# Issuing a phase's wide query product in one piece instead of one sixth per slot

## The reference, cut to what matters

```
q_hk  = (hidden_q @ Wq.T).reshape(B, S, 16, 128)
q_big = einsum('bshk,hkq->bshq', q_hk, w_kc_q)          # 192 wide per head
q_big = rope(q_big)
kv_r  = rope(kv_c)
q_r   = einsum('bshq,hqr->bhsr', q_big, W_qr)
k_r   = einsum('bld,hdr->bhlr', kv_r, W_kr)
attn  = softmax(einsum('bhsr,bhlr->bhsl', q_r, k_r))
ctx_c = einsum('bhsl,bld->bhsd', attn, kv_r)
out   = (ctx_c through w_kc_kv) @ Wo.T
```

## Time and profile before

| quantity | value |
|---|---|
| median of 3 runs | 955.08 us (953.51 to 961.84) |
| the profiled execution | 955.46 us |
| its span in the trace | 953.7 us, so 1.8 us lie around it |
| granted TensorE clock over the span | 0.93 |
| TensorE matmul busy | 847.4 us, 89% |
| VectorE, ScalarE, GpSimd busy | 61%, 44%, 47% |

### The profile page before, as it was taken

One profiled execution on the slowest core, in us unless ns is written; L12 is line 12 of the kernel. 1 busy time (PEld: TensorE's weight loads), 2 busy tenths in 40 slices (PEclk: granted clock), 3 DMA queues, 4 the chain that ended last, 5 costly groups with the idle time before them and its releaser, 6 DMA issues.

```text
span 953.7 us, 15582 instructions
## 1 busy us (share of the span) xinstructions
PE 847.4 (89%) x5844; PEld 629.2 (66%) x5844; DVE 582.8 (61%) x1112; ACT 415.9 (44%) x896; POOL 448.9 (47%) x465
## 2 busy tenths in 40 slices
PE   4998879989987799998989889899898988989884
PEld 3666756888965567766767667676676766766442
DVE  3537854222275567577587588668658748757445
ACT  2357851212121354544534544554454463454531
POOL 3000006500050187767657576666675755557530
PEclk8879989989997799999989999999999999999976
DMA  9560026589310000000000000010000000000000
GB/s 194 184 198 2 2 64 241 208 303 344 109 36 17 16 2 11 20 7 10 17 9 10 21 10 2 10 30 1 10 22 10 10 5 10 2 14 10 8 6 9
DMA packets 42167, 52.28 MB, mean 55 GB/s; under 512 B 12230, under 2 KB 35704, under 8 KB 41836
## 3 DMA queue, kind: packets, MB, share of 16 engines
q1 hardware_dynamic: 41068, 49.63, 16.6%
q0 software_dynamic: 1024, 1.64, 0.6%
HBM read 45.80 MB, written 5.36 MB: 54 GB/s over the span
## 4 chain that ended last, share of the span: by engine, by line
PE 68%; DVE 16%; ACT 7%; issue 4%; DMA 3%; POOL 1%; POOLq 0%; SPq 0%; DVEq 0%; ACTq 0%
PE ps L1167 13%; PE ps L1179 10%; PE ps L1147 7%; PE ps L1091 5%; PE ps L1015 5%; PE ps L1202 3%; PE ps L1118 3%; PE ps L969 3%; PE ps L1028 3%; PE ps L1096 2%; DVE nm L1931 2%; ACT sm L1424 2%; DMA xs<-xs_scratch 2%; DVE xyz L1902 1%; DVE h L1992 1%
## 5 line engine op out<-in xcount | busy, mean ns | idle before, releaser
L592 POOL TENSOR_TENSOR acc<-acc,pt 120x800 f32<-120x800 f32 (+1 forms) x157 | 301.6, 1921 | 123.5 <-ACT pt L1631 91.3
L1631 ACT ACTIVATE pt<-ps 120x400 f32<-120x400 f32 (+1 forms) x384 | 189.4, 504 | 237.1 <-PE ps L1167 229.4
L1931 DVE TENSOR_REDUCE nm<-ps 128x1 f32<-128x482 f32 (+1 forms) x336 | 215.7, 655 | 109.0 <-PE ps L1147 105.7
L1167 PE MATMUL ps<-qh,khl 128*120 128x400 f32 (+1 forms) x384 | 167.9, 437 | 24.0 <-ACT pt L1631 23.6
L1147 PE MATMUL ps<-khl,qh 128*128 128x482 f32 (+1 forms) x336 | 136.1, 408 | 10.6 <-DVE nm L1931 9.1
L1179 PE MATMUL ps<-pt,kv 120*64 120x400 f32 (+1 forms) x768 | 145.0, 514 | 0.0
L1167 PE MATMUL ps<-ql,kh 65*120 65x400 f32 (+1 forms) x384 | 137.2, 357 | 0.0
L1167 PEld LDWEIGHTS ps<-qh,khl 128*120 128x120 f32 (+1 forms) x384 | 72.9, 190 | 70.6 <-ACT pt L1631 34.3
L1179 PEld LDWEIGHTS ps<-pt,kv 120*64 120x64 f32 (+1 forms) x768 | 52.8, 140 | 66.6 <-issue 58.3
L614 POOL TENSOR_TENSOR rstd<-veps,mhalf 100x1 f32<-100x1 f32 (+2 forms) x19 | 13.0, 682 | 167.5 <-DVE veps L1765 115.4
L1091 PEld LDWEIGHTS ps<-x3T,wqb 128*128 128x128 f32 x512 | 76.6, 195 | 6.7 <-DVE xyz L1902 1.7
(11 more groups left out here) (273 smaller groups left out, 1270.5 us busy)
## 6 DMA issues: line engine op xcount, KB each, us to landing
egu<-_L_ffn_gate_up_proj_dram SPq DMA_DIRECT2D x14, 1024.0 KB, 6.0
edn<-in_L_ffn_down_proj_dram SPq DMA_DIRECT2D x14, 512.0 KB, 6.8
spread<-inv_scratch SPq DMA_DIRECT2D x30, 100.0 KB, 2.7
craw<-in_ctx_dram SPq DMA_DIRECT2D x8, 360.0 KB
wo_n<-in_L_xattn_Wo_dram SPq DMA_DIRECT2D x1, 2048.0 KB, 11.3
wq_n<-in_L_xattn_Wq_dram SPq DMA_DIRECT2D x1, 2048.0 KB, 8.0
xs_scratch<-zero SPq DMA_DIRECT2D x1, 1792.0 KB, 9.8
xs<-xs_scratch SPq DMA_DIRECT2D x14, 128.0 KB, 5.9
```

What stands on the lines that cost most here:

```text
L592: nc.gpsimd.tensor_tensor(total[r, :, :], before[r, :, :], pt[j % PT_BUF][r, :, :], ALU.add).then_inc(p_added, 1)
L1167: last = mm(ps[0:key_rows(t), k % 2, 0:HT], lhs[:, keys], rhs[:, HT * a:HT * a + HT], start=first, stop=not first)
L1631: nc.scalar.activation(pt[j % PT_BUF][0:rows, k % 2, :], ps[0:rows, k % 2, 0:HT], ACT.Exp).then_inc(p_ready, 1)
L1931: nc.vector.tensor_reduce(nm3[0:w, i, n:n + 1], ps[0:w, 3 + m % 2, 0:MN], AX.X, ALU.max).then_inc(m_reduced, 1)
```

## The change

The constant `QB_AT` is new, and the line that places the product now issues all six parts at slot 3 of the phase, one after the other. Nothing else changes: the same matmuls, the same waits, the same lists on the other engines. Because of the new line, all later lines have a number one higher.

```diff
+QB_AT = (3,)
...
-                    if u + 2 < NU and f < 2 and 1 <= x <= 6:
-                        q_big(u + 2, f, x - 1)
+                    if u + 2 < NU and f < 2 and x in QB_AT:
+                        for part in range(6):
+                            q_big(u + 2, f, part)
```

## The result

The changed kernel takes 985.43 us in the median of 4 runs (980.20 to 989.18), the kernel before 954.30 us in the median of 4 (946.16 to 961.84). The ratio is 1.0345 with a 95% interval of 1.0294 to 1.0395. So it is slower, as forecast, but by 31 us and not by 16, and 985.43 lies above the range of 960 to 983. The profiled execution took 989.18 us, the upper end of its four.

A forecast was written before the change was run, and what follows sets the result against it. The prediction took TensorE to bound the kernel, busy 89% of the span; its terms 3.1 + 2.1 + 4.7 + 1.4 + 2.1 + 1.8 + 1.0 = 16.2 us, on 955.46, gave 971.7 us, range 960 to 983.

The forecast's parts named there:

- Product in one piece: In each of 28 phases, one piece was to cost 0.11 us more than six parts: +3.1 us (2.5 to 4.2).
- Slot 2 of phase 0: At unit start, slot 2's scores wait for ScalarE's exponential until 1.23 us: 0.15 us by 14 units, +2.1 us.
- A late `low_q`: Odd units, slot 3: `max_chunk` waits for VectorE's late reduction, 0.88 us by 5, about 0.3 in sequence 1: +4.7 us.
- `turn_hq`: Slot 30 of the odd units with late `low_q`: TensorE waits for `keep_xq`, 0.28 us by 5, +1.4 us.
- `turn_keys` of slot 14: Phase 1 of even units, behind the piece: TensorE waits 0.3 us for `low_keys`, by 7 sequences, +2.1 us.
- slot 15 of odd units: Phase 1: `result` delays reduction 13, so slot 15's `max_chunk` waits 0.36 us, by 5, +1.8 us.
- `attention_out` behind `divide`: Nothing more for four units of five; unit 8's short 1.1 us wait may go: +1.0 us (0 to 1.7).
- slots 4 to 7 and 8 to 10 are covered: Reductions and exponentials nearly keep up there, and the piece or `values` lets them catch up: no cost priced.
- its clock unchanged: In the profile after, TensorE's clock was to stay the same; half-clock stretches coming or going were worth 1.7 us each.
- Cover holds: Rival: most small waits vanish, leaving the piece and late `low_q`, 3.1 to 7.5 us, about 960 us; chance 0.24.
- The piece is short: Rival: one piece takes 2.25 us instead of 2.70, -12.6 us over 28 phases, 942.9 us; chance 0.04.
- The clash grows: Rival: one more GpSimd add ahead of `divide` (9.4 us) and two more half-clock stretches (3.4 us), 984.5 us; chance 0.12.

The follow-up runs named there:

- fill_at1_at5: Changed kernel with the product at slot 1 in phase 0, slot 5 in phase 1, both long waits filled with repeated matmuls; 946.26 us, 0.9890 of before.
- before_fill: Kernel before, with harmless repeated matmuls filling TensorE's long waits at the table loads and at `divide`; 945.80 us, ratio to before 0.9909.
- after_fill: Changed kernel (piece at slot 3), with harmless repeated matmuls filling TensorE's long waits at the table loads and at `divide`; 969.08 us, ratio to before 1.0163.
- after_more_work: Changed kernel with every matmul of the down projection issued twice; 978.47 us, ratio to before 1.0260.
- both phases alone: Kernel before with the product in one piece at slot 3 in phase 0 only, 971.90 us (1.0168), or in phase 1 only, 964.94 us (1.0116).

## Why the prediction was right in direction and wrong in size

**The sum for the order was nearly right, in part by luck.** 16.2 us were forecast for the order and 18.9 measured at full clock (19.9 without the repeats of unit 8, 23.3 by the medians). But a term of 3.1 that isn't there stands against 5.8 of waits that were missing. By its terms:

- *Product in one piece*, +3.1: about zero. It takes 2.60 with 0.09 behind it, 2.69 against 2.70. (That fill_at1_at5 is no slower than before_fill doesn't show it, since its shorter waits for `divide` would hide such a cost.) I had read the two prologue pieces (2.76 and 2.70) as 24 equal records and then added the 0.09 of a part to them as well. The Trainium skill ("TensorE: Matmul & The Clock Gate", section LDWEIGHTS) has columns / 1.2 ns for a load, so 2.57 us for 24 loads (an estimate from it); the trace agrees with it to 0.03 in unit 6 and to 0.08 in unit 7.
- *Slot 2 of phase 0*, 1.23 us to its scores: exactly as worked out, 1.23.
- *A late `low_q`*: 1.00 to 1.03 us of marked wait, at the foreseen place, in the foreseen sequences, and 0.74 where it was to be smaller. In unit 9 the whole phase loses 1.19 of the 1.42 forecast. Part of the difference is a double count: the wait at slot 3 ends 3.45 us after the first scores in before and after alike, so in these five units the 0.15 of slot 2 lies inside it and can't be added (some 0.75 of the 2.1).
- *`turn_hq`* 0.22 against 0.28; *`turn_keys` of slot 14* 0.17 marked, 0.33 by the starts, against 0.3; *slot 15 of odd units* 0.11 marked and 0.28 by the starts in unit 9 of after_fill (688.68 - 687.81 - 0.59), against 0.36.
- *`attention_out` behind `divide`*, +1.0: the short wait of unit 8 is gone (1.11, now 2.88), and the marked time of the kind is 15.1 us in after against 13.1 in before, so 2.0, twice the forecast and a little above its upper bound of 1.7.
- What was missing: the start of a unit costs 0.39 and not 0.15 where no late `low_q` follows (unit 6), and light slots are 0.05 late for the exponential. I had written that slots 4 to 7 and 8 to 10 are covered. They nearly are. Without the 3.1 for the product the waits were forecast at 13.1, and 18.9 came, 5.8 more. Unit by unit, after_fill against before_fill, the odd units 5 to 13 lose 1.71 to 1.75 each, where the terms give 1.67; the even units 2, 4, 6, 10 and 12 lose 0.88 to 1.18, where they give 0.45, and unit 0 alone 1.66.

**The step that failed is "its clock unchanged".** TensorE lost some 14 us more to half-clock stretches in the profiled execution, 5 to 8 by the medians; by the medians the undersized waits, 23.3 against 16.2, are as large a part of the miss. I had priced such a stretch at 1.7 us from the earlier trace rows, but counted only waits that would be added: two, inside a rival of 0.12. What happened is that the waits that were already there, unchanged in length, were mostly followed by two stretches where they had had one or none. Half-clock time in the units went from some 38 to some 72 us. The filled waits show that this is the clock: filling them gave back 22.8 us of the units in after and 8.7 before. And after_more_work shows that it isn't the length of the wait. What decides between one stretch and two stays open.

**The rivals.** *Cover holds* is refuted by the result, 3.45% [2.94, 3.95], and by both phases alone, at 1.7 and 1.2%. *The piece is short* is refuted by 2.60 us. *The clash grows* had the right kind of loss and, by luck, almost the right time (984.5): the marked `divide` wait went up 2.0 us, not 9.4, and the clock took 14.1 and not 3.4.

**The sum.** 16.2 forecast; less 3.1 for the product, plus 5.8 for waits that were undersized or missed, is 18.9; plus 14.1 for the clock is 33.0, and 0.7 lie outside the units. This is for the profiled execution, whose 989.18 us lie 3.8 above the median.

## What to carry to other kernels

What it costs to issue a heavy block in one piece depends here on where it stands, at the same length: ahead of the place where the engine would wait anyway it fills the wait, and behind it, it leaves both the wait and slots too short for the other engines. An order also moves the other engines' steps against each other. Here a good part of the gain of one placement came from `divide` no longer running beside GpSimd's add, so look at these steps before a gain is put down to the block itself. When an order is compared, price the waits at full clock and the clock apart; filling the long waits of both kernels with repeated work that changes nothing is a quick way to see them apart, as long as one counts the repeats that fall into no wait. And count the long waits that a kernel already has, since an edit that only moves them in time can change what the clock does behind each.

## What the runs showed of the hardware that I had not expected

- Behind TensorE waits of 2.8 to 3.0 us (those for the table loads 3.00 to 3.03 in every kernel that isn't filled there) the clock was at half for none, 3.4 or 6.8 us. In the changed kernel it was 6.8 behind nine and ten of eleven, in the traces of two executions; adding 5 us of work removed half of it and made the kernel no slower.
- Filling those waits with repeated matmuls kept the mean granted clock at 1.00 over 560 to 580 us, and with them the kernel before took 0.9% less (0.9909).
- 24 f32 matmul records with their weight loads took 2.60 to 2.65 us in a stream at full clock, 0.108 to 0.110 each.
- `divide` took 0.57 us on VectorE when it started ahead of GpSimd's add, and 1.43 to 1.83 when it started during one; TensorE's wait behind it was 0.84 us in the one case and 2.80 to 2.89 in the other.
